# Three stages of a four-layer transformer kernel reordered at once, with extra identity multiplies in its tail

## What is computed

```python
x = x + L0_xattn(layernorm(x), ctx)     # 8-bit quantised q and k, one product, rank-one corrections
x = x + L0_ffn(layernorm(x))            # dense weight built from 4 bit planes and a table of 16, plus a bias
x = x + L1_xattn(layernorm(x), ctx)     # 16 heads over a latent space, softmax
x = x + L1_ffn(layernorm(x))            # int4 activations, ternary gate/up, relu^2, int8, ternary down
x = x + L2_xattn(layernorm(x), ctx)     # 32 heads of 128, 8 key/value groups, softmax
x = x + L2_ffn(layernorm(x))            # router of 64 experts, top 8: x*sum(w) + w @ expert_bias
x = x + L3_xattn(layernorm(x), ctx)     # top-k channel mask, features, 7-tap convolution, batch norm, gates
x = x + L3_ffn(layernorm(x))            # dense 512x512 + bias + top-2 of 8 rank-16 adapters
```

## Time and profile before

| | us |
|---|---|
| median of 3 runs | 984.63 (981.73 to 984.70) |
| the profiled execution | 985.47 |
| its span in the trace | 983.3 |

### The profile page before, as it was taken

One profiled execution on the slowest core, in us unless ns is written; L12 is line 12 of the kernel. 1 busy time (PEld: TensorE's weight loads), 2 busy tenths in 40 slices (PEclk: granted clock), 3 DMA queues, 4 the chain that ended last, 5 costly groups with the idle time before them and its releaser, 6 DMA issues. The chain is left out here.

```text
span 983.3 us, 16162 instructions
## 1 busy us (share of the span) xinstructions
PE 769.5 (78%) x4970; PEld 634.4 (65%) x4970; DVE 737.4 (75%) x1685; ACT 519.7 (53%) x1402; POOL 494.7 (50%) x416
## 2 busy tenths in 40 slices
PE   0375776855567889999999999999999997733257
PEld 0173565642236678889888988898898886621243
DVE  8984577866853779788788797887887978278653
ACT  5654576853413665755665657566756665120320
POOL 7870596004503275574664745836747466287000
PEclk9878899996779999999999999999999999875559
DMA  8233464018002021031210210311202201000021
GB/s 321 82 123 125 156 234 129 2 33 284 6 8 79 1 87 66 7 111 33 69 59 21 85 64 0 89 61 47 81 21 85 64 0 64 22 13 0 0 76 43
DMA packets 37510, 70.18 MB, mean 71 GB/s; under 512 B 5792, under 2 KB 14816, under 8 KB 37344
## 3 DMA queue, kind: packets, MB, share of 16 engines
q1 hardware_dynamic: 37472, 69.70, 21.2%
HBM read 64.35 MB, written 5.34 MB: 71 GB/s over the span
## 5 line engine op out<-in xcount | busy, mean ns | idle before, releaser
L1958 DVE TENSOR_SCALAR_CACHE_REDUCE xn<-ctxT,candidate 128x512 bf16<-128x512 f32 x248 | 174.5, 741 | 0.0
L1703 ACT ACTIVATE layer_attention_probs<-xnT,stats 128x512 f32<-128x512 f32 x128 | 94.1, 735 | 131.0 <-DVE stats L1808 130.9
L1498 PE MATMUL bank<-layer_attention_keysT,layer_attention_queriesT 128*128 128x512 f32 x384 | 121.5, 425 | 3.8 <-DVE layer_attention_queriesT L1801 3.8
L1820 DVE TENSOR_TENSOR layer_attention_probsT<-bank,layer_attention_probsT 128x512 fp32r<-128x512 f32 x128 | 88.2, 689 | 47.9 <-ACT layer_attention_probsT L1711 46.4
L1498 PEld LDWEIGHTS bank<-layer_attention_probsT,layer_attention_values 128*128 128x128 f32 x768 | 99.0, 189 | 16.1 <-DVE layer_attention_probsT L1820 6.2
L1498 PE MATMUL bank<-layer_attention_probsT,layer_attention_values 128*128 128x256 f32 x768 | 102.3, 282 | 7.6 <-DVE layer_attention_probsT L1820 7.0
L1498 PE MATMUL bank<-layer_attention_wo,layer_attention_headsT 128*128 128x512 f32 x384 | 103.4, 412 | 3.0 <-issue 3.0
L1711 ACT CAST layer_attention_probsT<-bank 128x512 fp32r<-128x512 f32 x128 | 74.8, 584 | 52.5 <-PE bank L1571 52.5
L1498 PE MATMUL bank<-layer_attention_l_wkv,layer_attention_l_ctxT 128*128 128x256 f32 x768 | 99.5, 283 | 1.4 <-PEq L1059 1.4
L1498 PEld LDWEIGHTS bank<-layer_attention_l_wkv,layer_attention_l_ctxT 128*128 128x128 f32 x768 | 97.1, 191 | 4.3 <-issue 1.9
L1498 PE MATMUL bank<-layer_attention_l_wq,layer_attention_xnT 128*128 128x512 f32 x384 | 93.3, 392 | 0.0
(11 more groups left out here) (291 smaller groups left out, 1745.5 us busy)
## 6 DMA issues: line engine op xcount, KB each, us to landing
layer_attention_l_raw_qo<-in_wqT SPq DMA_DIRECT2D x9, 1024.0 KB, 5.1
xnT<-inverse_sums SPq DMA_DIRECT2D x16, 512.0 KB, 3.6
layer_attention_l_raw_qo<-in_woT SPq DMA_DIRECT2D x8, 1024.0 KB, 6.8
tw_raw<-in_w_gateT SPq DMA_DIRECT2D x8, 688.0 KB, 4.8
tw_raw<-in_w_upT SPq DMA_DIRECT2D x8, 688.0 KB, 4.3
tw_raw<-in_w_downT SPq DMA_DIRECT2D x6, 768.0 KB, 4.7
layer_attention_l_raw_kv<-in_wkvT SPq DMA_DIRECT2D x9, 512.0 KB, 4.9
ternary<-tw_rounded SPq DMA_DIRECT2D x8, 344.0 KB, 2.5
```

The lines of the kernel that those rows point to most:

```text
L1498: last = pe.matmul(out, stationary[f][a], moving[f][b], start=f == 0 and x == 0, stop=f == count - 1 and x == 2)
L1703: a.activation(probs[:, u % 3, :], masked[:, u % 2, :], ACT.Exp, bias=negmax[:, u:u + 1], scale=-1.0, accum_out=sums[:, u:u + 1]).then_inc ...
L1820: v.tensor_tensor(probsT[:, 1, p % 2, :, columns], T[u % 2][:, :].rearrange("p (c q) -> p c q", c=CPB), probsT[:, 0, p % 2, :, columns], A ...
L1958: own(k.nc.vector.tensor_scalar(k.flags[:, r % 2], row_tile(k.ctxT, r), k.candidate[:, r:r + 1].bitcast(F32), 0.0, ALU.is_ge, ALU.add, acc ...
```

## The change

**layer0.** (1) All eight leaves of blocks 0 and 2 go to ScalarE, of block 1 to GpSimd; block 3 is shared, four leaves each. ScalarE begins with `leaves(0)`; x is rectified, rounded and coded ahead of the context. (2) The bias is loaded as one row and enters the product's banks as a one-row matmul (`add_bias`), before the products, which then accumulate on it; GpSimd's four additions fall away. (3) The row correction is one ScalarE activation from a precomputed `corr_base`, and x's tiles are corrected around the two column scalings. (4) `unpack(2)` moves from before the attention's additions to after the second norm's statistics, and `norm_rows` moves ahead of `choose(1)`. (5) The ternary sums are spread: pieces 0 to 2, then 3, then 4 and 5 before `weightT_copy(3)`, 6 and 7 after it; SUMMED_EARLY = 8, so piece 8 is summed at the start of layer1_attention.

**layer1_ffn.** The norm goes tile by tile (`tile_norms_vector`, `tile_norms_gpsimd`); the row sums of absolute values go to ScalarE; the int4 quantisation goes by halves; and TensorE's order becomes the one at the end of this section, with the down product of a tile as soon as it was turned.

**Tail.** The blocks layer2_ffn, layer3_attention, layer3_ffn and epilogue become one block `tail`. Its norms go tile by tile, with the update of x of a tile just ahead of its statistics. `band` comes ready-made from the host as an input. All loads are issued at the block's start. Only `choose_channels(0)` stands before the softmax, the other three stand after the second norm. The softmax's division is left to the end (top-8 of the exponentials; the mix is scaled by `total`). The parts of layer 3 are made by batch. The dense product runs in three one-pass products of high and low parts (`xnT2`, `wb`, fp32r), whose weight GpSimd splits after the second norm's powers; ScalarE and VectorE split `xnT`. The output is stored tile by tile. `plain` is written over the context in place.

**Warm-up matmuls.** TensorE's program of the tail gets 148 matmuls of the 128 x 128 bf16 identity by itself (512 columns each) into a bank that is not in use:

```diff
+                def keep_busy(bank, count):
+                    for _ in range(count):
+                        pe.matmul(k.bank[bank][:, :], k.ident16[:, :],
+                                  k.ident16[:, :].unsqueeze(1).broadcast_to([P, KT, P]), start=True, stop=True)
...
+                keep_busy(7, 16)
+                for t in range(TILES):
+                    turn(0, t)
+                for t in range(TILES):
+                    expert_logits(t)
+                keep_busy(7, 28)
+                pe.wait_ge(S_["dense_ready"], 1)
...
+                keep_busy(3, 10)
+                for t in range(TILES):
+                    turn(1, t)
+                pe.wait_ge(S_["x_mixed"], TILES)
+                keep_busy(7, 64)
+                pe.wait_ge(S_["band_loaded"], 48)
+                pe.wait_ge(S_["features_ready"], 1)
...
+                keep_busy(7, 20)
+                for t in range(TILES):
+                    pe.wait_ge(S_["gated_ready"], KT * (t // TPB + 1))
...
+                keep_busy(3, 10)
+                turn(2, 0)
+                turn(2, 1)
...
+                pe.wait_ge(S_["wb_low"], 1)
+                pe.wait_ge(S_["parts_low"], TILES)
+                pe.wait_ge(S_["x_gated"], TILES)
+                for t in range(TILES):
+                    dense_product(t)
```

```diff
+def tile_norms_vector(k, n, ready=None):
...
+    stats(0)
+    stats(1)
+    aggregate(0)
+    stats(2)
+    variance(0)
+    aggregate(1)
+    stats(3)
+    variance(1)
+    aggregate(2)
+    rows(0)
+    variance(2)
+    aggregate(3)
+    rows(1)
+    variance(3)
+    rows(2)
+    rows(3)
...
                 norm_statistics(k)
+                unpack(2)
+                norm_rows(k, n + 1)
                 choose(1)
-                norm_rows(k, n + 1)
                 unpack(3)
...
                 weightT_copy(0)
-                leaves(1)
-                for i in range(0, 4):
+                for i in range(0, 3):
                     ternary_sums_scalar(k, i)
+                leaves(2)
                 for t in range(TILES):
                     a.wait_ge(k.xnT_in_psum, TILES * m + t + 1)
...
                 weightT_copy(1)
-                leaves(3)
+                ternary_sums_scalar(k, 3)
+                leaves(3, 4)
                 weightT_copy(2)
-                for i in range(4, TernaryWeights.SUMMED_EARLY):
+                for i in range(4, 6):
                     ternary_sums_scalar(k, i)
                 weightT_copy(3)
+                for i in range(6, TernaryWeights.SUMMED_EARLY):
+                    ternary_sums_scalar(k, i)
...
+                gate_up(0)
+                turn4(2)
+                turn4(3)
+                gate_up(1)
+                turn8(0)
+                gate_up(2)
+                down(0)
+                turn8(1)
+                gate_up(3)
+                down(1)
+                turn8(2)
+                down(2)
+                turn8(3)
+                down(3)
...
+                tile_norms_gpsimd(k, n0 + 1)
+                g.wait_ge(S_["wb_loaded"], 16)
+                g.tensor_copy(wb[:, 0], raw_wb[:, :, :]).then_inc(S_["wb_high"], 1)
+                g.wait_ge(S_["wb_high"], 1)
+                g.tensor_tensor(wb[:, 1], raw_wb[:, :, :], wb[:, 0], ALU.subtract).then_inc(S_["wb_low"], 1)
...
+                tile_norms_vector(k, n0 + 1, mixed)
+                for r in (2, 4, 6):
                     choose_channels(k, r)
```

More of the change, by code:

```diff
@@ new lines, in turn @@
+                def turn(n, t):
+                    pe.wait_ge(k.tile_xn, TILES * (n0 + n) + t + 1)
+                    if t >= 2:
+                        pe.wait_ge(S_["turned"], TILES * n + t - 1)
+                        if n == 2:
+                            pe.wait_ge(S_["parts_low"], t - 1)
+                    for f in range(KT):
+                        last = pe.transpose(T[t % 2][:, f * P:(f + 1) * P], k.xn[:, t, f * P:(f + 1) * P], k.ident[:, :])
+                    last.then_inc(S_["turned_psum"], 1)
@@ new lines, in expert_logits @@
+                def expert_logits(t):
+                    if t == 0:
+                        pe.wait_ge(S_["router_loaded"], 48)
+                    pe.wait_ge(S_["turned"], t + 1)
+                    for f in range(KT):
+                        last = pe.matmul(k.bank[2][:, t * EXPERTS:(t + 1) * EXPERTS], k.xnT[:, f, t * P:(t + 1) * P],
+                                         router[:, f, :], start=f == 0, stop=f == KT - 1)
+                    if t == TILES - 1:
+                        last.then_inc(S_["logits_psum"], 1)
@@ new lines, in _ @@
+                pe.wait_ge(S_["features_ready"], 1)
+                for j, (blk, c) in enumerate((blk, c) for blk in (1, 0, 2) for c in range(2)):
+                    first, end = max(0, 1 - blk), min(KT, KT + 1 - blk)
+                    last = pe.matmul(k.bank[2][:, first * 4:end * 4], band[:, c, blk, :],
+                                     features[:, c, first + blk - 1:end + blk - 1].rearrange("p f r b -> p (f r b)"),
+                                     start=j == 0, stop=j == 5)
+                last.then_inc(S_["z_psum"], 1)
@@ L2481, in build @@
             run(layer1_ffn, layer2_attention)
-        run(layer2_ffn, layer3_attention, layer3_ffn)
-        epilogue(k, out)
+        k.out = out
+        run(tail)
 def layout(inputs):
```

825 lines of the change are left out of this document (409 added, 416 removed).

## The result

The changed kernel takes 958.3 us (median; 955.0 to 959.8) against 984.4 us of the kernel before in the same comparison, a ratio of 0.9737 [0.9706, 0.9767]: 26 us faster. The forecast was 951 us, with a range from 940 to 962, so the time lies inside the range and 7 us above the point. The profiled execution took 955.02 us, 1.7 us more than its span, and is the fastest of the four shown.

A forecast was written before the change was run, and what follows sets the result against it. Untouched layer2_attention, over half the span, keeps TensorE busy; the other stages examined were taken as chains of waits. Gains of 5.4, 11.2 and 17.0 us from 985.47 gave 951.9, stated as 951, range 940 to 962.

The forecast's parts named there:

- The sum: Whole kernel: gains of 5.4, 11.2 and 17.0 us, together 33.6, taken from the profiled execution's 985.47 us, giving 951.9.
- The tail's addition: Tail's end: last update at 963.7 plus 2.4 us for the store, given as 966.3 against 983.3, gain 17.0.
- the mechanism: layer0's end: ScalarE's last copy no longer waits behind five sums and runs at 75.2 instead of 81.0, gain 5.8 us.
- the collision of the choice with GpSimd's split: layer0's end: VectorE's last choice waits about 3.2 us for GpSimd's subtraction, with the last turn at 74 to 74.5.
- the step that failed: layer1_attention's start: the sum handed over costs ScalarE 1.5 us, mostly hidden; 0.4 us taken of 0 to 1.5.
- my 5.0: Tail, before the parts: VectorE's choices lose 5.0 us to GpSimd's split of `wb` (bounds 0 and 7).
- the split of `xnT`: Tail, behind `xn`: ScalarE copies and VectorE subtractions make a 5.2 us chain (bounds 3 and 7), 942.5 to 947.7.
- The run of 20: Tail, ahead of the back-transposes: 20 warm-up matmuls take 6.6 us, against 5.05 us of idling, ending 1.5 us late.
- Rival c: Tail: warm-up matmuls end up on the path; slower than before only from 34 us uncovered, at most 1016; chance 0.02.
- (a): layer0, layer1_ffn and tail: GpSimd's long subtractions miss VectorE's steps, saving 3.2, 2 and 5 us: 941 us; chance 0.25.
- (b): TensorE's new chains late: dense product up to 4 us, down products 3, layer0's last product 2: 960 us; chance 0.23.
- a sign of a wrong prediction: layer2_attention, which the change does not touch: its time off 567 us by over 2 would show the prediction wrong.

The follow-up runs named there:

- g0: The kernel before with the new one-block tail alone; 972.1 us, ratio 0.9878 to before.
- f2: The kernel before with the new layer1_ffn alone; 972.0 us, ratio 0.9872 to before.
- e2: The changed kernel with nine instead of eight ternary pieces summed early in layer0; 958.5 us, ratio 0.9717 to before.
- f1: The kernel before with the new layer0 alone, eight early sums included; 984.4 us, ratio 0.9989 to before.
- e4: The changed kernel with GpSimd's split of the latent weights moved from layer0's end into layer1_attention, behind its norm's powers; 952.0 us, ratio 0.9657 to before.
- e3: The changed kernel with the split of `wb` late: ScalarE makes the high part, GpSimd subtracts behind the last gated product; 954.6 us, ratio 0.9676 to before.

## Why the prediction was right where it was, and wrong where it was not

**The sum.** The sign, the size and the range were right. Against its own yardstick, the profiled execution, the forecast said 951.9 and the profile gave 955.0. Part of the remaining gap to the median is the yardstick: the profiled execution of before was 0.8 us above its median, that of the changed kernel 3.3 below. One profile of each is worth some 3 us either way here, and the sum of the terms pretended to be finer than that. The tail's addition also slips by 0.2 us: 963.7 and 2.4 are 966.1, not 966.3.

**layer0: the mechanism was right, one term was mis-sized.** The copy no longer stood behind the sums (it ran at 76.61, and TensorE waited 0.67 us instead of 6.16). What had held it in the kernel before was not only the summing but also the loads of the pieces: ahead of its last three sums ScalarE waited 2.71, 1.79 and 1.78 us for them. With the same code that copy came at 78.81 in g0 and 79.66 in f2, not at 81.00: the trace that I forecast from was the latest of the three. I had said a last turn at 74 to 74.5; it was 75.45, because the collision of the choice with GpSimd's split cost 4.8 us (9.47 against 4.63), not 3.2; GpSimd's step itself took 6.63 us instead of the 4.54 of the earlier trace rows, so both stood still for a time. With TensorE idle for 4.87 us ahead of it, the turn and the product also ran longer (5.97 us instead of 5.68). The stage gained 4.1 us by these two traces (2.3 to 5.1 by all), not 5.8.

**layer1_attention: the step that failed.** I priced the piece handed over at one sum of 1.5 us on ScalarE, of which I took 0.4. Its load was left out, though the description of the kernel before says that piece i+2 is loaded into the buffer that piece i leaves. The two buffers make each load wait for the sum two pieces earlier; with the ninth sum moved behind the block's end, the eleventh piece's load was issued behind it, and ScalarE stood 3.24 us ahead of the copies that TensorE needs. Then TensorE, idle for 3.40 us, ran the latent product in 5.37 us instead of 3.67, which g0 shows can also happen without that wait. 4.3 us against 0.4 (3.5 to 4.6 in the six traces with that order); in e2 TensorE's longer wait and the slow product are gone, and f1 shows that the whole of layer0's change is worth nothing measurable without a cure. The remedy that paid was not e2's but e4's.

**layer1_ffn: right.** The first gate and up product came 10.6 us after the stage's start (10.0 forecast: 227.4 against 217.35), set by the load, as said. The second 8-bit step, not the first, met GpSimd's 5.02 us subtraction, and the third tile's last chunk was at 260.89, 42.1 us into the stage (42.3 forecast: 259.6). The last update ended 62.5 us in (281.22; 64.0 forecast, 281.4), so the stage did some 1.5 us better than the sum:

```profile
229.36 5.87 PE L1309 MATMUL bank<-layer_ffn_wgu,layer_ffn_x4T 128*128 128x512 bf16 x23 [1.34 <-DMA layer_ffn_wgu<-ternary]
```

```profile
251.16 5.06 DVE L1239 TENSOR_SCALAR layer_ffn_inner<-layer_ffn_inner 128x1376 f32<-128x1376 f32 x1
...
280.47 0.75 DVE L1250 SCALAR_TENSOR_TENSOR x<-bank,layer_ffn_down_scale,x 128x512 f32<-128x512 f32 x1 [3.21 <-PE bank L1322]
```

```profile
250.48 5.02 POOL L1399 TENSOR_TENSOR layer_attention_l_wq<-layer_attention_l_raw_qo,layer_attention_l_wq 128x2048 fp32r<-128x2048 f32 x1
```

They answer to the earlier trace rows. f2 confirms the size, 13.8 us by medians.

**The tail: right, for reasons that nearly cancel.** Up to the parts it gained 9.8 us (920.27 and 896.59 lie 59.4 and 49.6 us behind the first statistics step), where I had 8.0; the collision cost 5.1 of my 5.0. Behind it, the first rows of `xn` came 8.8 us after the gates (914.81 to 923.60) instead of 10.9, and I had said 9.9. The chain behind `xn` was mis-sized the other way. I gave the split of `xnT` 5.2 us (bounds 3 and 7) and the dense product's start at its end; from the last row's end, 926.4, to 933.84 it was 7.5 us. The third and fourth tile's turns wait for VectorE's split of the first and second and stand in TensorE's queue among the low-rank products (929.80), and those took 5.5 us in all. TensorE was indeed the late one: from 930.66 on it had no wait but the 0.68 us for `lowT`. The dense product took 11.39 us (10.6 forecast), and the store was over 2.5 us after the last addition ended, at 950.78 (2.4 forecast).

The Trainium skill (SBUF — State Buffer, Who interferes with whom) also says that a `tensor_scalar` that writes its accumulator out does not contend, and that a VectorE step with at most one SBUF input outside the two-port modes does not. The traces agree with both: of the steps of one choice, the one with the accumulator took its 0.73 us in the middle of GpSimd's subtraction while the plain one behind it took 3.93, and in e3 the additions from PSUM kept 0.69.

**The warm-up products.** "Each buys only what the work right behind it saves" held: 0.9 to 2.7 us in the tail as built. The run of 20 was the tight one, as forecast (6.6 us long; measured 6.08 to 7.04 in five traces). Rival c needed 34 us uncovered to make the kernel slower than before; 148 products more cost 3 to 6 us: VectorE's own work covered most of them, and those that overran gave something back to the work they reached (1.2 us in the convolution, 1.4 in the low-rank products, 4.04 us against 5.46).

**The other rivals.** (a) did not happen anywhere: the two long subtractions of the tail and of layer0, and the one of layer1_ffn, all met VectorE. (b) happened in layer0's last product and in the low-rank products, about 2 us in all, not in the dense product. What I had named as a sign of a wrong prediction, layer2_attention off its 567 us by more than 2, came true between the same steps (565.2 against 567.8) and proved nothing: the sign was set finer than the executions agree.

## What to carry to other kernels

When a step is handed to the next stage, follow its buffer: the load behind it moves too, and it may be worth more than the step (here 1.5 us handed over, 3.5 to 4.6 lost). A long GpSimd step that reads SBUF belongs beside VectorE work that reads PSUM or waits, and the gain of moving it can be read beforehand off the durations, alone and beside (5.1 us for the split of `wb`, and that came). Warm-up products pay when each run ends at the moment the real work comes; as they stood they were worth 1 to 3 us, fitted to the waits they were worth 6, and doubled they cost 3 to 6.

## What the runs showed of the hardware

Predicated copies lose time beside GpSimd's cast and two-input subtraction of 128x2048, as VectorE's other steps did: three of them (128x2048, 128x1024, 128x512) took 4.63 us alone and 9.47 beside the pair, and the subtraction took 6.63 us instead of 4.58 (its time in e4, beside the rows of a norm). Four `pow` steps on 128x1 take GpSimd 2.84 us, 0.71 each, against 1.01 for one on 128x4; tile norms pay that for their early start. The same program's executions differ by up to 9 us (953.2 to 962.3), more than most single edits here, so single parts were read from stages and only the larger ones from medians; and a stage with the same code differs by 1 to 6 us between traces (layer0 87.3 to 88.7, the new tail 106.3 to 108.1, layer2_attention 564.7 to 570.4).
